# Maxima of the attention scores from four 32-row matmuls into four banks, with the work of a head group dealt out anew

## What is computed

```
q = layernorm(x) @ w_q + b_q;  k = context @ w_k + b_k;  v = context @ w_v + b_v    # 16 heads of 32
scores = einsum('bqhd,bkhd->bhqk', q, k) / sqrt(32)
out = einsum('bhqk,bkhd->bqhd', softmax(scores, axis=-1), v)
x = x + out @ w_o + b_o
```

## Time and profile before

| | us |
|---|---|
| median of 3 runs | 1717.89 |
| lowest, highest | 1717.18, 1721.56 |
| the profiled execution | 1716.18 |
| its span in the trace | 1713.9 |
| PE busy | 1576.5 (92%) |
| DVE busy | 1225.9 (72%) |
| ACT busy | 1128.4 (66%) |
| POOL busy | 1023.3 (60%) |

### The profile page before, as it was taken

How to read it: one execution, slowest core, us unless ns; L and a number is a source line. 1 busy time by engine, 2 the same in 40 slices (tenths; PEclk the granted TensorE clock), 3 DMA queues, 4 the chain that set the end, 5 groups by cost and what they waited for, 6 DMA issues and landing times. The chain is left out here.

```text
span 1713.9 us, 29296 instructions
## 1 busy us (share of the span) xinstructions
PE 1576.5 (92%) x8836; PEld 711.7 (42%) x8836; DVE 1225.9 (72%) x1756; ACT 1128.4 (66%) x1895; POOL 1023.3 (60%) x738
## 2 busy tenths in 40 slices
PE   5999878998999977999999999999999978999998
PEld 3545433444444432334344443444343413444443
DVE  4978898997989745776776767676767666665553
ACT  5667598887888744665656666666656566566562
POOL 4767437766677723565667566665757565554452
PEclk9989999999999997999999999999999999999999
DMA  8411000000000112121211212121211100010001
GB/s 313 143 66 42 1 1 1 1 1 1 0 1 1 62 52 73 33 59 26 58 33 38 54 29 57 26 57 32 58 25 40 55 25 25 25 49 24 24 24 49
DMA packets 61230, 72.21 MB, mean 42 GB/s; under 512 B 15312, under 2 KB 40784, under 8 KB 60624
## 3 DMA queue, kind: packets, MB, share of 16 engines
q1 hardware_dynamic: 56944, 62.22, 12.3%
q10 hardware_dynamic: 4192, 8.92, 1.3%
HBM read 37.40 MB, written 8.39 MB: 27 GB/s over the span
## 5 line engine op out<-in xcount | busy, mean ns | idle before, releaser
L1556 DVE TENSOR_REDUCE s_mx<-bank 128x1 f32<-128x512 f32 x512 | 336.9, 685 | 193.9 <-PE bank L1684 188.0
L1443 ACT ACTIVATE s_E<-bank 128x512 f32<-128x512 f32 x512 | 293.8, 595 | 195.4 <-PE bank L1696 171.9
L1342 POOL TENSOR_TENSOR s_E<-s_E 128x1024 f32<-128x1024 f32 x128 | 300.3, 2367 | 123.7 <-PE bank L1704 116.6
L1684 PE MATMUL bank<-s_KA,s_QA 96*128 96x512 f16 x512 | 193.3, 388 | 20.7 <-DMA s_KA<-sm_cx 10.4
L1696 PE MATMUL bank<-s_QA,s_KA 97*128 97x512 f16 x512 | 195.7, 384 | 3.9 <-ACT s_E L1443 1.4
L1335 POOL TENSOR_TENSOR sm_cx<-s_qkf,sm_cx 128x512 f16<-128x512 f32 x64 | 76.4, 1194 | 171.3 <-ACT sm_cx L1421 171.2
L1865 POOL TENSOR_TENSOR sm_cx<-m_xf,sm_cx 128x512 f16<-128x512 f32 x60 | 84.1, 1407 | 105.0 <-ACT sm_cx L1907 105.0
L1704 PE MATMUL bank<-s_E,s_V 128*32 128x512 f32 x1024 | 135.6, 602 | 3.9 <-ACT s_E L1443 3.9
L1075 PE MATMUL bank<-sm_zz,w1raw 128*128 128x512 f16 x256 | 99.7, 389 | 28.4 <-DVE sm_cx L962 15.4
L1098 PE MATMUL bank<-f_w2q,w2raw 128*128 128x512 f16 x512 | 121.8, 379 | 0.6 <-DVE w2raw L950 0.3
L772 POOL TENSOR_TENSOR sm_wkv<-sm_wkv,sm_cx 128x511 f32<-128x511 f32 x48 | 66.2, 1380 | 89.8 <-DVE sm_wkv L962 80.5
(11 more groups left out here) (264 smaller groups left out, 4055.1 us busy)
## 6 DMA issues: line engine op xcount, KB each, us to landing
sm_cx<-in_ctx SPq DMA_DIRECT2D x16, 768.0 KB, 4.6
s_QA<-sm_cx SPq DMA_DIRECT2D x384, 32.0 KB, 1.9
s_KA<-sm_cx SPq DMA_DIRECT2D x372, 32.0 KB, 1.9
X<-in_x SPq DMA_DIRECT2D x8, 1024.0 KB, 6.7
out_x<-X SPq DMA_DIRECT2D x8, 1024.0 KB, 4.3
w1raw<-in_w ACTq DMA_DIRECT2D x1, 4096.0 KB, 13.9
w2raw<-in_w ACTq DMA_DIRECT2D x1, 4096.0 KB, 27.3
w1raw<-in_wq SPq DMA_DIRECT2D x1, 1024.0 KB, 5.4
```

What stands on the lines that cost most here:

```text
L1342: e.tensor_tensor(into, into, other, ALU.add).then_inc(s_sum.sem, 1)
L1443: e.activation(E[:, SLOT[k] + h, :], SC[u % 2][:, :], ACT.Exp, scale=1.0 / float(np.sqrt(DH)))\
L1556: e.tensor_reduce(mx[:, h, q:q + 1], MX[q % 2][:, :], AX.X, ALU.max).then_inc(s_red.sem, 1)
L1684: e.matmul(MX[k % 2][:, :], QA[0:MROW, m, h, q * P:(q + 1) * P], KA[0:MROW, m, h, :], start=True, stop=True).then_inc(s_mx.sem, 1)
```

## The change

Maxima. All four heads of a query tile q are done at once: four matmuls of 32 rows each, straight from the high halves of q and k (partitions 32 h to 32 h + 31) into four banks (banks 0 to 3, so the two score banks too), one semaphore count for the four, then four reduces on VectorE, one a bank. The three-part stack is not needed for them. A group has four such steps, at units 0, 4, 8 and 12 of the phase before; each waits for all exponentials so far, since it overwrites the score banks, and the first two scores behind it wait for the reduces of banks 0 and 1. `qkh` is double-buffered.

The row of maxima. `rows` moves from unit 15 of the phase before to the start of the phase itself, and the DMA from ScalarE's queue to SyncE's, where it stands ahead of this phase's two stacks and so behind the stacks of the phase before.

Work dealt out anew. q is projected in units -1 to 3 and taken by ScalarE after unit 3 (before: at the start of the phase), k after unit 7, in phase 2 after unit 11; the values of groups 2 and 3 move to phase 0, those of the next batch's groups 0 and 1 to phase 3; the output projection goes over phases 1 and 2 with eight products each; the reciprocals are spread; GpSimd adds the last pair of tiles of a group in the next phase.

The core of the diff:

```diff
-    K_UNITS = (SPARSE_K, (-1, 0, 1), (2, 3, 4), SPARSE_K)
-    V_UNITS = (SPARSE_V, (12, 13, 14, 15), SPARSE_V, SPARSE_V)
-    T_UNITS, STATS_UNITS = (4, 6, 8, 10), (1, 3, 6, 10)
-    MAX_AHEAD = 2
-    PV_UNIT, DN_LATE = (6, 10, 14), 6
+    Q_AT = ((-1, -1, 1, 3), (-1, -1, 1, 3), (0, 1, 2, 3), (0, 1, 2, 3))
+    K_AT = ((3, 5, 7), (5, 7, 7), (7, 7.5, 11), (3, 3.5, 5))
+    V_AT = ({2: (7, 7.5, 9, 11), 3: (11.5, 11.5, 13, 15)}, {}, {}, {0: (7, 7, 9, 11), 1: (11, 11.5, 13, 15)})
+    T_AT = (9, 11, 13, 15)
+    O_AT = ({}, {3: ((0, 0),), 7.5: ((0, 1),), 11: ((0, 2), (0, 3)), 11.5: ((1, 0),), 13: ((1, 1),), 15: ((1, 2), (1, 3))},
+            {3: ((2, 0),), 5: ((2, 1),), 7: ((2, 2),), 9: ((2, 3),), 11: ((3, 0),), 11.5: ((3, 1),), 13: ((3, 2),), 15: ((3, 3),)},
+            {})
+    DN_TILE, AN_AT = (1, 1, 1, 2), 12
+    EARLY_RC = {4: (0,), 8: (1, 2), 12: (3,)}
...
         @block.sync
+            def maximum_row(b, m):
+                s_mrow.wait(e, b, m + 1)
+                s_sc.wait(e, b, 16 * (m + 1) - 16 * NG)
+                e.dma_start(QA[MROW:MROW + 1, m, :, :].rearrange("o h (q n) -> o (h q) n", n=P), mrow[:, :])\
+                    .then_inc(s_md[m].sem, 16)
             def step(b, m, first, last):
                 proj = what(b, m, first, last)[0]
                 if m == 0 and not last:
                     context(b + 1)
+                maximum_row(b, m)
                 if proj:
                     stack(e, *proj, 0)
                     stack(e, *proj, 1)
...
         @block.scalar
+                rows(b, m)
...
                 for u in range(UNITS):
                     exponential(b, m, u)
...
+                    if proj and u == 3:
+                        queries(*proj, 0)
+                    if late and u == 7 and m == 1:
+                        divided(*late)
+                    if proj and u == (11 if m == 2 else 7):
                         queries(*proj, 1)
...
         @block.vector
+            def maxima(b, m, q):
                 s_mT.wait(e, b, m)
+                s_mx.wait(e, b, TT * m + q + 1)
+                for h in range(4):
+                    e.tensor_reduce(mx[:, h, q:q + 1], MX[h][:, :], AX.X, ALU.max).then_inc(s_red.sem, 1)
...
         @block.tensor
+            def maxima(b, m, q):
+                if q == 0:
+                    e.wait_ge(s_qkh.sem, s_qkh.count(b, 2 * m + 2))
                     s_mrow.wait(e, b, m)
+                s_red.wait(e, b, 4 * (TT * m + q))
+                high = qkh[m % 2]
+                for h in range(4):
+                    head = slice(h * DH, (h + 1) * DH)
+                    last = e.matmul(MX[h][:, :], high[head, 0, q * P:(q + 1) * P], high[head, 1, :], start=True, stop=True)
+                last.then_inc(s_mx.sem, 1)
...
+                for u in range(UNITS):
+                    t, h = divmod(u, 4)
+                    if nxt and h == 0:
+                        if t == 0:
+                            s_mrow.wait(e, b, m + 1)
+                        e.wait_ge(s_ex.sem, s_ex.count(b, 16 * m + 4 * t))
+                        maxima(*nxt, t)
+                    if t and h == 0:
+                        attend(b, m, t - 1)
+                    if div and u == 0:
+                        attend(*div, TT - 1)
+                        denominators(*div, 0)
+                    if div and u == 4 * DN_TILE[m]:
+                        denominators(*div, 1)
+                    between(u - 0.5)
+                    score(b, m, u, nxt)
+                    between(u)
```

More of the change, by code:

```diff
@@ L1356, in step @@
             def step(b, m, first, last):
-                proj, nxt, div = what(b, m, first, last)
+                proj, nxt, div, late = what(b, m, first, last)
+                if div:
+                    summed(*div, 1, 0)
+                if m == 3:
+                    divided(b, 0)
+                if div:
+                    summed(*div, 1, 1)
+                if last and m == 3:
+                    divided(b, 1)
+                if m == 2 and not last:
+                    context(b + 1)
                 if proj:
-                    if m == 2:
-                        context(b + 1)
                     low(*proj, 0)
+                summed(b, m, 0, 0)
+                if m == 1 and late:
+                    divided(*late)
+                if m == 2:
+                    summed(b, m, 0, 1)
+                if proj:
                     low(*proj, 1)
@@ L1486, in step @@
             def step(b, m, first, last):
-                proj, nxt, div = what(b, m, first, last)
-                if m == 2 and not last:
-                    for c in range(KC):
-                        context(b + 1, c)
-                if proj:
-                    queries(*proj, 0)
-                if div and N_UNIT[m] < 0:
+                proj, nxt, div, late = what(b, m, first, last)
+                rows(b, m)
+                if first and m == 0:
+                    e.wait_ge(s_lo, 2)
+                    e.wait_ge(s_raw[3], 32)
@@ L1494, in step @@
+                if m == 0 and not first:
+                    values(b, 1)
+                if m == 1:
+                    values(b, 3)
+                if m == 2 and not last:
+                    context(b + 1, 0)
+                    context(b + 1, 1)
+                if m == 3:
+                    divided(b, 0)
+                elif div:
                     numerators(*div)
+                if m == 2 and not last:
+                    context(b + 1, 2)
                 for u in range(UNITS):
-                    if u == UNITS - 1 and nxt:
-                        rows(*nxt)
@@ L1741, in step @@
             def step(b, m, first, last):
-                proj, nxt, div = what(b, m, first, last)
+                proj, nxt, div, late = what(b, m, first, last)
                 if m == 0:
-                    reader[6], reader[7] = (s_V, b, 2), (s_qkf, b, 4)
-                if m == 2 and nxt:
-                    for k in range(MAX_AHEAD):
-                        maximum(*nxt, k)
-                if proj:
-                    for c in range(KD):
-                        queries(*proj, 0, c)
@@ L1785, in step @@
                             output(b, q, c, END_BANK[q], True)
+                if proj and Q_AT[m][0] < 0:
+                    queries(*proj, 0, 0)
+                rows(b, m)
+                if first and m == 0:
+                    s_V.wait(e, 0, 2)
+                    e.wait_ge(s_lo, 2)
+                between(-1)
+                for u in range(UNITS):
[15 more added lines that the diff above has]
+                    between(u)
             for m in range(2):
@@ L1794, in _ @@
                     values(0, m, t, m)
-            for k in range(UNITS):
-                maximum(0, 0, k)
-            rows(0, 0)
             s_V.wait(e, 0, 2)
-            e.wait_ge(s_lo, 2)
+            for q in range(TT):
+                maxima(0, 0, q)
             steps(step, e)
```

234 lines of the change are left out of this document (105 added, 129 removed).

## The result

| | before | after |
|---|---|---|
| median (lowest to highest) | 1717.5 us (1715.9 to 1721.6) | 1832.8 us (1827.7 to 1840.1) |
| span of the profiled execution | 1713.9 us | 1828.5 us |
| ratio to before, 95% interval | | 1.067 (1.0627 to 1.0714) |

The change makes the kernel 115 us slower. The prediction had the sign, and 1769 us; the time lies above its range of 1712 to 1800.

The account below looks back on a forecast made before the run. TensorE was taken as the bound before. SyncE's queue and tiles give 98.7 us a batch, 3.0 for the clock 101.7: +8.0 in seven batches (+56), ends -5, 1767, as median 1769 us; range 1712 to 1800.

Parts of the forecast that it names:

- the landing of the row in phase 0: Phase 0: the DMA of the row of maxima lands 1.7 us after its issue, as in other phases.
- the clock in phase 0: Phase 0 start: no slowdown charged; a fall to 1.2 GHz was charged only in phase 3, at 3.0 us.
- the tiles of phase 1: Phase 1: its chains of maxima, reduces, scores and exponentials, with TensorE's other work, set its length, 25.0 us.
- the two ends: First and last batch: fewer waits for stacks and less work make them together 5 us shorter (-10 to 0).
- TensorE's load: Maximum matmuls: four 32-row matmuls run side by side at 0.36 us a set, saving TensorE 8.1 us a batch.
- Rival (c): Sets of maxima: the 32-row matmuls run one after the other, +25 us, 1795 us; chance 0.08.
- The walk of tiles without the queue: All four phases, if the row comes in time: 22.2, 25.0, 22.6 and 22.5 us, together 92.3 a batch.
- The upper bound: Phase 1: at most 25.9 us, where transposes in units 11 and 15 wait for VectorE's reduces and reciprocals.
- The queue: SyncE: the row waits behind the previous phase's stacks, 0.62 us an issue; phases become 22.7, 25.0, 26.6, 24.4 us.
- The sum: Whole kernel: seven batches at +8.0 us give +56, beginning and last batch -5, from 1716.2 to 1767 us.
- (b): SyncE: its queue is not in the way, or costs were counted too dear; 1702 us, chance 0.15.
- (d): All phases: tiles at their bare chain and no fall of the clock, 93.3 us a batch, 1712 to 1718; chance 0.07.

Follow-up runs that it names:

- the kernel with all three edits: Changed kernel with the row's DMA issued by ScalarE, phase 1's reciprocals later and its normalisations in units 0 to 3: 1702.6 us, ratio 0.9931.
- the first experiment: Changed kernel with the DMA of the row of maxima issued by ScalarE again instead of SyncE: 1724.8 us, ratio 1.0058.
- the useless matmuls: Changed kernel with 20 unneeded matmuls in phase 0 and 12 in phase 3 during TensorE's wait for the row: 1807.1 us, ratio 1.0546.

## Why the prediction was wrong

The sign and the mechanism held; three terms of the sum were too small (the landing of the row in phase 0, the clock in phase 0, the tiles of phase 1), and the two ends had the wrong sign.

**TensorE's load.** Right: the row form was taken at 0.36 a set, and attend starts 0.33 after it. The Trainium skill's 0.28 ("TensorE: Matmul & The Clock Gate", Measured speedup vs the span model) leaves 0.05 of it for the change of form; nothing hung on it. Rival (c), 1795, had the nearest time and the wrong reason: the four matmuls are one row of 0.40 us.

**The walk of tiles without the queue.** Right in sum: 22.2, 25.0, 22.6, 22.5 against 21.7, 25.5, 23.3, 22.3 in the kernel with all three edits, 92.3 against 92.7. But after itself is not that kernel. In phase 1, 28.4 us without the queue, the walk had four reduces and two reciprocals ahead of the rounding and took 25.0 between 22.7 and 25.9. It left out that VectorE's normalisation stands while GpSimd adds, and that the clock falls in phase 1 (0.94; in the one middle batch of the first experiment where it stays at 1.00 the phase takes 27.3 us). The upper bound was too low by 2.5 us. That tiles and not the queue bind phase 1 was forecast and holds in after: from the row at 1119.72 to the end of the k stack at 1142.46 SyncE takes 22.7 us, the number forecast for it, and the next row goes out 6.0 us later. This is the third failing step: 25.0 were forecast, 26.7 to 28.7 measured from row to row, some 20 us in seven batches.

**The queue.** The mechanism was right and named in all its parts: the row behind the twelfth k issue, 0.62 an issue, idle at the start of phase 3 (3.5 us for 4.1), lower clock there. From row to row the phases were predicted at 22.7, 25.0 (the tiles), 26.6 and 27.4 with the clock; the issues of the row at 1092.58, 1119.72, 1148.44, 1175.66 and 1203.86 are 27.1, 28.7, 27.2 and 28.2 apart. Phases 2 and 3 are within 0.8. In phase 0 these two steps failed:

- *The landing.* 1.7 us was taken everywhere, though the row that it came from shows a longest one of 5.1. That one stood 0.1 us behind a load of 1024 KB. In phase 0 it is 4.0 to 4.5, behind the context load, which the change put directly ahead of it. Its issue was priced (0.4) and its 768 KB were not. +2.5 us in phase 0; 17 to 20 us in the time.
- *The clock.* It was charged to phase 3 alone. The same reasoning, idle time by the chain and then the lower clock, wasn't carried to the start of phase 0, where TensorE stands 5.45 us and the rows are 0.63 as well. From the first score to the end of exponential 3 it is 3.9 us there, 2.7 with the useless matmuls, and from there to the first issue of the stack 3.4 for 2.9: +1.8 us. The 3.0 charged to phase 3 were 2.7 in the batch shown (6.4 us to the end of exponential 3 for 3.7) and 1.5 to 1.7 in the others. In phases 0 and 3 together the clock is worth 22 to 26 us.

So 8.0 us more a batch were predicted, and it was 16.

**The sum.** Seven batches were charged 8.0 each, and the two ends were taken at -5. The six middle batches are 14.7 to 17.7 us longer than those of before, the first 20.3, more than any other, and the last 2.4. What lies in front of the first mark (from the context load that the stage begins with) is 2.1 us shorter, 60.2 for 62.3, and what lies behind the last mark, to the last product with the exponentials, 3.6 longer, 35.7 for 32.1. So the ends cost some 4 us where 5 were to be gained.

**Rivals.** (b) and (d) are what the kernel would have been without the queue and with phase 1 repaired: 1702.6 us measured where (b) said 1702. That the two meet so closely is luck: (b) stood 16 us below the kernel before, and this is 10 below. As a forecast of this change (b) fell for the reason given: 12 issues took 7.47 us. The range ended at 1800 since (c) was its upper case; none of its cases let two terms of the likeliest be wrong together in the same direction.

## What to carry to other kernels

Before a DMA that an engine waits for is moved to another queue, write down what is ahead of it there at that moment: the issues (0.62 us each here), when the data of the last one come, and how large the transfer just ahead is, in this queue or another. Where such a chain sets a loop's period, work saved on the busiest engine gives nothing, and each small delay in the loop (landing, clock, a stalled instruction) is paid in full, so price them in every phase and not only in the one that looks worst. If the first fix doesn't bring the time back, look at which phase kept its length: here 10 us above before hid a second fault of 3 us a batch, and with it repaired the reordering was worth 10 us, 0.7%.

## What the runs showed of the hardware

**A small DMA behind a large one.** The row of maxima, 4 KB, lands after 1.7 us, and after 4.0 to 4.5 when 768 KB were issued 0.7 us ahead of it in the same queue. With the order turned round, no landing is over 1.7. Another queue is no shelter: with the row on ScalarE's queue and 1024 KB issued on SyncE's ahead of it, it lands after 5.1 us (0.1 us behind, the kernel before) and 3.8 (2.1 us behind).

**Issue time.** 12 issues of 32 KB take SyncE 7.47 to 7.50 us, before and after. The Trainium skill ("Trainium Kernel Development and Optimization", Key Constraints) says that issuing from several engines only saves the sequencer's issue time. The traces agree that it is the place among the issues that counts: a second engine took the row from 1833 to 1725 us, and another order on one engine to 1727. With what hangs on it (landing, clock) that "only" is some 105 us here.

**VectorE beside GpSimd.** A normalisation of 128x512 takes 0.54 us and up to 2.60 while GpSimd adds 128x1024. The Trainium skill ("SBUF — State Buffer", Terms) says that the two share a port pair that one instruction holds until its end, the other being blocked and not slowed. The traces agree: in after such a normalisation ends 0.3 us behind GpSimd's sum in all eight batches.

**The clock.** It fell not only after idle stretches of 3.5 and 5.5 us but in phase 1 too, whose longest shown wait is 1.93 us, and there in some batches and not in others of the same kernel with the same waits (26.3 us at 1.00, 28.0 at 0.94). What tips it there stays open.
